# Layer-norm shift products of a cross-attention block: one column per product against one row of 512 columns

## The reference

```python
q, kv = _ln(queries, q_norm_g, q_norm_b), _ln(tokens, kv_norm_g, kv_norm_b)
qp = q @ in_proj_w[:D].T + in_proj_b[:D]
kp = kv @ in_proj_w[D:2*D].T + in_proj_b[D:2*D]
vp = kv @ in_proj_w[2*D:].T + in_proj_b[2*D:]
scores = einsum('bhld,bhtd->bhlt', qh, kh) / sqrt(hd) - spatial_scale * dist + spatial_offset
attn_out = einsum('bhlt,bhtd->bhld', softmax(scores), vh)
x = queries + attn_out @ out_proj_w.T + out_proj_b
h = gelu(_ln(x, mlp_norm_g, mlp_norm_b) @ mlp_w1.T + mlp_b1)
x = x + h @ mlp_w2.T + mlp_b2
```

## Time and profile before

| | us |
|---|---|
| median of 3 runs | 1252.32 (1252.31 to 1252.36) |
| the profiled execution | 1252.47 |
| its span, first to last instruction | 1250.6 |
| PE busy | 1220.2 (98%) |
| PE weight loads | 819.0 (65%) |
| DVE busy | 993.6 (79%) |
| ACT busy | 851.3 (68%) |
| POOL busy | 992.0 (79%) |

### The profile page before, as it was taken

One profiled execution on the slowest core, in us unless ns is written; L12 is line 12 of the kernel. 1 busy time (PEld: TensorE's weight loads), 2 busy tenths in 40 slices (PEclk: granted clock), 3 DMA queues, 4 the chain that ended last, 5 costly groups with the idle time before them and its releaser, 6 DMA issues.

```text
span 1250.6 us, 27744 instructions
## 1 busy us (share of the span) xinstructions
PE 1220.2 (98%) x9424; PEld 819.0 (65%) x9424; DVE 993.6 (79%) x2656; ACT 851.3 (68%) x1914; POOL 992.0 (79%) x1286
## 2 busy tenths in 40 slices
PE   9888988999999999999999999999999999999998
PEld 6656455666667666666666676666666666666664
DVE  5799998888878888888888989888888787778321
ACT  5867757676877677676767677776767677676331
POOL 5478897989898898989898998989898987767320
PEclk9788999999999999999999999999999999999999
DMA  6699999888999898998999998998889897879543
GB/s 185 197 188 208 224 224 195 192 189 209 209 194 222 180 214 198 193 203 201 198 205 218 180 223 182 202 203 203 194 206 208 195 208 176 173 170 180 142 113 123
DMA packets 468686, 241.69 MB, mean 193 GB/s; under 512 B 384048, under 2 KB 408896, under 8 KB 468544
## 3 DMA queue, kind: packets, MB, share of 16 engines
q1 hardware_dynamic: 468544, 239.91, 85.6%
HBM read 109.66 MB, written 12.58 MB: 98 GB/s over the span
## 4 chain that ended last, share of the span: by engine, by line
PE 86%; DVE 8%; issue 2%; ACT 1%; POOL 1%; DMA 1%; SPq 0%; POOLq 0%; DVEq 0%; ACTq 0%
PE ps_up L630 26%; PE ps_down L645 26%; PE ps_qk L566 12%; PE ps_vo L590 6%; PE ps_vo L587 6%; PE ps_s L601 5%; PE ps_pv L615 4%; DVE p_nat L1071 1%; DVE soft L1054 1%; PE ps_down L510 1%; DVE w L999 1%; DVE w L1005 1%; DVE x_nat L1031 1%; PE ps_down L541 0%; DVE qk_parts L1045 0%
## 5 line engine op out<-in xcount | busy, mean ns | idle before, releaser
L1248 POOL TENSOR_SCALAR p_nat<-soft,row_inv 128x256 f16<-128x256 f32 x512 | 332.1, 658 | 61.2 <-DVE row_inv L1065 59.4
L630 PE MATMUL ps_up<-hT,w 128*128 128x256 f16 x3072 | 377.2, 273 | 3.1 <-ACT u L805 2.7
L645 PE MATMUL ps_down<-w,hid 128*128 128x512 f16 x1536 | 372.9, 379 | 0.8 <-DVE hid L1103 0.4
L630 PEld LDWEIGHTS ps_up<-hT,w 128*128 128x128 f16 x3072 | 300.3, 98 | 93.2 <-ACT u L805 3.2
L773 ACT ACTIVATE soft<-soft,neg_max 128x256 f32<-128x256 f32 x512 | 255.2, 500 | 117.2 <-DVE neg_max L1054 116.2
L1054 DVE CUSTOM_DVE_ANT_0 soft<-ps_s,soft,factor 128x256 f32<-128x256 f32 x512 | 225.4, 476 | 116.7 <-PE ps_s L601 115.9
L1071 DVE SCALAR_TENSOR_TENSOR p_nat<-soft,row_inv,p_nat 128x256 f16<-128x256 f32 x512 | 297.6, 620 | 2.1 <-POOL p_nat L1248 1.9
L1256 POOL TENSOR_SCALAR soft<-dist,scale_neg,offset 128x512 f32<-128x512 f32 x256 | 244.3, 954 | 14.0 <-DVE p_nat L1071 13.6
L645 PEld LDWEIGHTS ps_down<-w,hid 128*128 128x128 f16 x1536 | 148.6, 97 | 132.4 <-DMA w<-x_scratch 1.4
L805 ACT ACTIVATE u<-ps_up,bias,up_scale 128x256 f32<-128x256 f32 x256 | 142.3, 556 | 124.9 <-PE ps_up L630 121.5
L1264 POOL TENSOR_SCALAR hid<-u,hid_scale 128x1024 f16<-128x1024 f32 x64 | 77.3, 1208 | 105.0 <-ACT u L811 105.0
(11 more groups left out here) (122 smaller groups left out, 1569.5 us busy)
## 6 DMA issues: line engine op xcount, KB each, us to landing
w<-x_scratch SPq DMA_DIRECT2D x256, 256.0 KB, 3.1
stack<-qk_parts SPq DMA_DIRECT2D x256, 96.0 KB
raw<-in_ctx SPq DMA_DIRECT2D x32, 256.0 KB, 3.4
raw<-in_x SPq DMA_DIRECT2D x32, 256.0 KB, 3.1
c_stage<-in_w SPq DMA_DIRECT2D x32, 256.0 KB, 3.6
x<-in_x SPq DMA_DIRECT2D x32, 256.0 KB, 3.5
out<-x SPq DMA_DIRECT2D x32, 256.0 KB, 3.2
tok_rows<-in_tok_xy SPq DMA_DIRECT2D x16, 256.0 KB, 4.4
```

Source lines behind the costliest of these rows:

```text
L630: mm = e.matmul(ps_up[s % 2][:, 0:L], w_1_sb[:, wp, k, m * P:(m + 1) * P], hT[:, b % 2, :, xp * KT + k, :], start=(k, wp, xp) == (0, 0, 0) ...
L645: mm = e.matmul(ps_down[tt][:], hid[:, chunk % HID_RING, i, hp, tt * P:(tt + 1) * P], w_2_sb[:, s % W2_RING, wp, :], start=(m == 0 and (hp ...
L1248: mine = e.tensor_scalar(p_nat[:, nat, HI, lc, :], soft[:, ring, lc, :], row_inv[:, ring, lc:lc + 1], 1.0, ALU.mult, ALU.mult)
```

## The change

It makes the shift products as rows. The stationary operand is now the single column of shifts, the moving operand is the whole 512-column weight row of one 128-row quarter, and the result is one row of 512 outputs. K, Q and V take 4 products each instead of 16, the MLP weight 16 instead of 64; the MLP chunks' rows lie on partitions 0, 32, 64 and 96 of their bank. The columns are read in the order of `by_column`, a step of 128 numbers between neighbours, so that the four numbers of one partition stand together in the row. ACT copies the row to SBUF (`bias_row`, `bias_rows_1`), and a DMA scatters it over the 128 partitions (`bias_turn`, `bias_turn_1`), from where DVE reads it as before. The row tiles lie in memory that other tiles use, and so `dist_square` and `load_residual` gain a wait for the scatter.

V's shift product moves from slots -2, 0 and 2 to slot -3, DVE's step for the MLP bias from slot 19 to 21. The unread products are placed anew: `warm` makes 10, 1, 1, 12 and 6 products instead of 10, 3, 10, 8, 2 and 8, and `keep_busy` starts in slot 0 instead of 7, writes `ps_pv` before slot 9, and counts a shift-product step as 4 units instead of 8. One more unread product (`clear_rows`) writes the MLP rows' bank in slot 0.

```diff
+        row_kv = sb("row_kv", [1, D], F32, at["x1"] + KT * D * 4)
+        row_q = sb("row_q", [1, D], F32, at["x1_n"])
+        rows_1 = sb("rows_1", [P, D], F32, at["x1"] + (KT + 1) * D * 4)
...
+            def bias_turn(sec):
+                gate.wait_ge(s_row, AT[sec] + 1)
+                e.dma_start(bias_qkv[:, sec * KT:(sec + 1) * KT], (row_q if sec == SEC_Q else row_kv)[:]).then_inc(s_rowd[sec], DMA)
+
+            def bias_turn_1():
+                gate.wait_ge(s_row, ROW_1)
+                for c in range(N_CHUNKS):
+                    e.dma_start(bias_1[:, c * CH:(c + 1) * CH], rows_1[32 * c:32 * c + 1, :]).then_inc(s_rowd_1, DMA)
...
-                gate.wait_ge(s_mkept, DMA)
-                gate.wait_ge(s_colsum, 1)
+                if t >= KT:
+                    gate.wait_ge(s_rowd_1, N_CHUNKS * DMA)
...
+                for sec, at_slot in ((SEC_K, -25), (SEC_Q, -24), (SEC_V, -1)):
+                    if slot == at_slot:
+                        bias_turn(sec)
+                if slot == 18:
+                    bias_turn_1()
...
-            def weight_bias(sec, quarters):
+            def by_column(w):
+
+                return w.rearrange("p (m q) -> p q m", m=KT)
...
                 gate.wait_ge(s_cols, DMA)
                 b_ln = B_Q if sec == SEC_Q else B_KV
-                for k in quarters:
...
-                    for m in range(KT):
-
-                        col = sec * KT + m
-                        mm = e.matmul(ps_bias[sec][:, col:col + 1], w_stage[sec][:, k, m * P:(m + 1) * P],
-                                      cols_sb[:, b_ln + k:b_ln + k + 1], start=((k, m) == (0, 0)), stop=((k, m) == (KT - 1, KT - 1)))
-                if KT - 1 in quarters:
...
+                if sec == SEC_V:
+                    gate.wait_ge(s_row, ROW_K)
                 for k in range(KT):
-                    mm = e.matmul(ps_bias[sec][:, col:col + 1], w_stage[sec][:, k, m * P:(m + 1) * P],
-                                  cols_sb[:, b_ln + k:b_ln + k + 1], start=(k == 0), stop=(k == KT - 1))
-                if m == KT - 1:
-                    mm.then_inc(s_brow)
...
-            def w1_bias(c, m):
-                col = c * CH + m
-                for k in range(KT):
-                    gate.wait_ge(s_wc[c % C_STAGES][k], n_staged(c))
-                    mm = e.matmul(ps_bias_1[:, col:col + 1], staged(c, k)[:, m * P:(m + 1) * P],
-                                  cols_sb[:, B_M + k:B_M + k + 1], start=(k == 0), stop=(k == KT - 1))
-                if m == CH - 1:
+                    if sec == SEC_V:
+                        gate.wait_ge(s_w[0], DMA)
+                    else:
+                        gate.wait_ge((s_wk if sec == SEC_K else s_wq)[k], DMA)
+                    mm = e.matmul(ps_bias[sec][0:1, :], cols_sb[:, b_ln + k:b_ln + k + 1], by_column(w_stage[sec][:, k, :]),
+                                  start=(k == 0), stop=(k == KT - 1))
+                mm.then_inc(s_brow)
+
+            def w1_bias(c, k):
+
+                gate.wait_ge(s_wc[c % C_STAGES][k], n_staged(c))
+                mm = e.matmul(ps_bias_1[32 * c:32 * c + 1, :], cols_sb[:, B_M + k:B_M + k + 1], by_column(staged(c, k)),
+                              start=(k == 0), stop=(k == KT - 1))
+                if k == KT - 1:
                     mm.then_inc(s_brow)
...
+            def clear_rows():
+
+                e.matmul(ps_bias_1[:], w_sec[SEC_K][:, HI, 0, 0:P], w_sec[SEC_K][:, HI, 0, :], start=True, stop=True)
...
-            def keep_busy(count):
-
-                gate.wait_ge(s_bo_all, 1)
+            def keep_busy(bank, count):
+
+                if bank is ps_down[0]:
+                    gate.wait_ge(s_bo_all, 1)
+                gate.wait_ge(s_wlo, AT[SEC_K] + 1)
                 for _ in range(count):
-                    e.matmul(ps_down[0][:], w_sec[SEC_K][:, HI, 0, 0:P], w_sec[SEC_K][:, HI, 0, :], start=True, stop=True)
...
+                    e.matmul(bank[:], w_sec[SEC_K][:, HI, 0, 0:P], w_sec[SEC_K][:, HI, 0, :], start=True, stop=True)
...
-                for at_slot, count in ((-32, 10), (-30, 3), (-8, 10), (-6, 8), (-3, 2), (-2, 8)):
+                for at_slot, count in ((-32, 10), (-30, 1), (-28, 1), (-8, 12), (-6, 6)):
...
-                for sec, quarters, at_slot in ((SEC_K, range(3), -31), (SEC_K, range(3, KT), -29), (SEC_Q, range(1), -29),
-                                              (SEC_Q, range(1, 3), -28), (SEC_Q, range(3, KT), -27)):
+                for sec, at_slot in ((SEC_K, -31), (SEC_Q, -29), (SEC_V, -3)):
                     if slot == at_slot:
-                        weight_bias(sec, quarters)
-                for m, at_slot in enumerate((-2, 0, 2, 2)):
-                    if slot == at_slot:
-                        value_bias(m)
+                        weight_bias(sec)
+                if slot == 0:
+                    clear_rows()
                 if slot == 4:
                     value_bias_out()
...
-                if 7 <= slot < DOWN:
+                if 0 <= slot < DOWN:
                     taken = 1 + (3 if due(slot, 9, GROUP, N_HG) else 0) + (6 if slot % 2 else 0) + (6 if slot >= UP else 0)
-                    taken += vo_done + (8 if due(slot, 1, ITEM, MT) else 0)
-                    keep_busy(max(0, SLOT_STEPS - taken))
+                    taken += vo_done + (4 if due(slot, 1, ITEM, MT) else 0)
+                    taken += 16 if slot == 4 else 0
+                    keep_busy(ps_pv if slot < 9 else ps_down[0], max(0, SLOT_STEPS - taken))
...
-                gate.wait_ge(s_bcol, BIAS_Q)
+                gate.wait_ge(s_row, ROW_Q)
...
+            def bias_row(sec):
+                gate.wait_ge(s_brow, AT[sec] + 1)
+                if sec == SEC_V:
+                    gate.wait_ge(s_rowd[SEC_K], DMA)
+                e.activation((row_q if sec == SEC_Q else row_kv)[:], ps_bias[sec][0:1, :], ACT.Copy).then_inc(s_row)
+
+            def bias_rows_1():
+                gate.wait_ge(s_brow, 3 + N_CHUNKS)
+                gate.wait_ge(s_mkept, DMA)
+                gate.wait_ge(s_colsum, 1)
+                e.activation(rows_1[0:97, :], ps_bias_1[0:97, :], ACT.Copy).then_inc(s_row)
...
+                gate.wait_ge(s_rowd[SEC_Q], DMA)
...
+                for sec, at_slot in ((SEC_K, -26), (SEC_Q, -24), (SEC_V, -2)):
+                    if slot == at_slot:
+                        bias_row(sec)
+                if slot == 17:
+                    bias_rows_1()
...
-                gate.wait_ge(s_brow, AT[sec] + 1)
-                e.tensor_tensor(bias_qkv[:, part], ps_bias[sec][:, part], cols_sb[:, B_IN + sec * KT:B_IN + (sec + 1) * KT], ALU.add).then_inc(s_bcol)
+                gate.wait_ge(s_rowd[sec], DMA)
+                e.tensor_tensor(bias_qkv[:, part], bias_qkv[:, part], cols_sb[:, B_IN + sec * KT:B_IN + (sec + 1) * KT], ALU.add).then_inc(s_bcol)
...
-                gate.wait_ge(s_brow, 3 + N_CHUNKS)
-                e.tensor_tensor(bias_1[:], ps_bias_1[:, 0:MT], cols_sb[:, B_1:B_1 + MT], ALU.add).then_inc(s_bcol)
+                gate.wait_ge(s_rowd_1, N_CHUNKS * DMA)
...
-                if slot == 19:
+                if slot == 21:
                     bias1_columns()
```

More of the change, by code:

```diff
@@ L967, in bias_v_spread @@
             def bias_v_spread():
-                gate.wait_ge(s_brow, AT[SEC_V] + 1)
+                gate.wait_ge(s_rowd[SEC_V], DMA)
                 gate.wait_ge(s_wsq, WSQ[3])
                 part = slice(SEC_V * KT, (SEC_V + 1) * KT)
-                e.tensor_tensor(bias_qkv[:, part], ps_bias[SEC_V][:, part], cols_sb[:, B_IN + SEC_V * KT:B_IN + (SEC_V + 1) * KT],
+                e.tensor_tensor(bias_qkv[:, part], bias_qkv[:, part], cols_sb[:, B_IN + SEC_V * KT:B_IN + (SEC_V + 1) * KT],
                                 ALU.add).then_inc(s_tv)
```

12 lines of the change are left out of this document (4 added, 8 removed).

## The result

| | before | after |
|---|---|---|
| median of the runs, us | 1252.34 (4 runs, 1252.31 to 1255.13) | 1260.1 (4 runs, 1259.58 to 1260.6) |
| ratio, 95% interval | | 1.0056 (1.0039 to 1.0074) |
| the profiled execution, its span | 1252.47, 1250.6 | 1260.6, 1258.8 |
| granted clock, mean of the span | 0.986 | 0.997 |

The change makes the kernel slower by 0.56%, some 7.8 us. I had forecast 5 us less, and the result lies above my range.

The account below looks back on a forecast made before the run. Chained waits bound the start, DVE's pace 58 to 176 us, PE the rest. Start 2.4 plus slots 2.6 gave 5.0 us off 1252.47, and with the median 0.15 lower 1247.3 us; range 1242.5 to 1255.0.

Parts of the forecast that it names:

- Prices: Cost of one 512-column row product on PE, taken from L541: 0.9 us at full clock, 1.8 at half.
- Rival (2): PE's stepped read halves the stream, 1.8 us a product even at full clock: slower, 1254.8 us; chance 0.15.
- The MLP rows: Rival (2)'s term for w1 steps: 0.9 us more each, 14 in all, of which 0.4 was counted.
- The start: Before slot 0: the forecast gained 2.4 us; Rival (2) lost 4.2, from K and Q 1.6 and V 2.6.
- the slots' gain: Slots 0 to 30: 2.6 us in the forecast, of which Rival (2) kept 2.1.
- The clock rises during the first product: K's rows at 6.2 us: PE's clock rises in their first product, so four take 4.5 us, done at 10.7.
- Rival (1): Narrow rows do not raise PE's clock; the start loses 1.6 us, the slots keep 2.1: 1251.8 us; chance 0.20.
- No 0.50 after 50 us: Sign that the forecast is right: PE's granted clock never reads 0.50 after 50 us.
- V's rows, 3.6 us at full clock: V's rows, ahead of a K projection that started at 33.9 us: 3.6 us, hidden; at 7.2 not hidden.
- What is late next is the scatter: ACT's `dist_square` waits for Q's scatter, landing at 20.2 to 22.9 us; Q's high parts start at 22 to 24.6.
- the slots' 2.6: Slots 0 to 30: 1.8 at O's total, 1.2 at the bias, 0.6 other idleness, less 1.0 for unread products.
- rival (3): DVE, 96% busy from 58 us, eats the slots' gain, leaving 0.4 beside the start's 2.4: 1249.5 us; chance 0.15.

Follow-up runs that it names:

- Experiment 1: Changed kernel with all weight rows read in natural order, ACT's row copy making the scatter's order; 1249.04 us, ratio 0.9970 to before.
- experiment 4: Measurement in the changed kernel: MLP weight chunks read with steps of 1, 2, 4, 8 numbers, unread fp16 products with steps up to 128; 1271.43 us, one run.
- experiment 9: Measurement in the changed kernel: MLP weight chunks and unread fp16 products read in 16-byte steps or short runs with jumps, one chunk plain; 1263.44 us, one run.
- experiment 5: Changed kernel with only K's, Q's and V's rows in natural order, the MLP weight's rows still stepped; 1253.61 us, ratio 1.0006 to before.
- experiment 8: Experiment 1 with Q's row in memory not otherwise used then, so `dist_square` does not wait for its scatter; 1248.71 us, ratio 0.9964 to before.
- experiment 10: Experiment 1 with `keep_busy` starting in slot 7 instead of 0; 1249.85 us, ratio 0.9977 to before.
- Experiment 7: Experiment 1 with 26 unread products instead of 6 in slot -6, ahead of Q's projection; 1247.28 us, ratio 0.9953 to before.

## Why the prediction was wrong

**The step that failed is in "Prices".** "Of the new form ... no row exists. Its bounds: half of that at the lower end ..., twice as much at the upper. I take 0.9 and 1.8, the nearest row." At full clock the upper bound was the true value: 1.78 us a product where the sum has 0.9, and nearly all rows ran at full clock. The form differed from the nearest row, L541, in two things, the narrow stationary operand and the step of the moving one. Experiment 1 shows that the first is free (0.90 to 0.91 us a product), experiments 4 and 9 that with the second each number costs a line of its own. With the natural order the same change gives -3.8 us of the -5.0 forecast.

**Rival (2) named the mechanism, and its sum was too small by 5.3 us** (1254.8 against 1260.1). The Trainium skill (SBUF — State Buffer, Door 1: The DMA port swizzle) says that a 16-byte line is what a read pays for, and that at least two hits a line keep it free. The trace agrees with the line as the unit. Two hits a line are free here in fp32 (1.06 against 1.02) but not in fp16 (0.47 against 0.24). The same section of the Trainium skill gives figures for a free stride, 4 numbers in fp32 and 8 in bf16 (fp16 here, of the same width). They don't hold for PE's moving operand here either: a step of 4 in fp32 doubles the product (1.96 against 1.02), and in fp16 already a step of 4 does.

The rival's prices failed in two terms, which make 4.5 of the 5.3 us:
- The MLP rows. I counted 0.4 of 14 us, because "PE had 9 us free in 58 to 122 and gets more by the clock". They cost 4.3 (experiment 5 against 1). The 14 us were right, (1.90 - 1.02) x 16; but these slots also hold the unread products, which fill each slot to 16 units, and the table counts a step as 4 units, 0.96 us. PE was busy 57.91 of 64 us with plain rows, 6 us free and not 9 or more, and the 14 us went into that stretch and little around it. The free time of the kernel as changed was what the price had to be held against.
- The start. I counted 4.2 lost and it was 4.8 against before, and 8.0 against experiment 1 (46.36 against 38.40; 6.1 to 8.0 over experiments 1, 5, 8 and 10, whose K, Q and V rows are plain). K's rows take 3.4 us more than plain (7.12 - 1.02 - 2.73), Q's 3.5 and V's, which stand ahead of a K projection, 2.7; of these 9.6 us 8.0 reach slot 0.

The rival also kept 2.1 us of the slots' gain. Up to the first MLP product it did not come (see below).

**The clock, point by point.** "The clock rises during the first product" was right or a little late. Where the ten unread products still take 4.45 us (experiments 7 and 8), K's rows take 3.71 and 3.81 against 3.59 at full clock, so the rise falls into their first product; in after (4.25) and in experiment 1 (3.63) it came already during the ten. That it also rises during one-column-wide rows is shown by V's, in after and in experiment 1. Rival (1) falls. "No 0.50 after 50 us" was right as well (1.00 in both stretches). What I had not seen is the place between K's and Q's projections, where PE waits 5.2 us for DVE and the clock falls: Q's projection at 2.72 instead of 1.47 us and V's rows partly at half speed. My "V's rows, 3.6 us at full clock" took no account of it. Experiment 7 fills the wait, and both run at full clock again.

**The start's chain.** With plain rows the foretold places are nearly met: "the copy of Q's total at 16 to 17 us" was 15.85, `dist_square` behind the scatter at 20.47 lies inside "20.2 to 22.9", and the start gains 3.15 us where I had 2.4. That agreement is weak: the scores of slot 0 stand at 38.40, 38.88, 40.24 and 39.22 us in experiments 1, 5, 8 and 10, and at 41.55 and 39.95 in two executions with the columns, so one profile can't place the start's gain. But "What is late next is the scatter" was wrong: experiment 8 takes its wait away and nothing moves. DVE's chain of Q's gain, norm and low parts is late there. The scatter of Q's row landed after 2.0 us in after and 3.3 with plain rows, where I had 2.3 to 5.0.

**Slots 0 to 30.** "DVE's wait at 44 us below 2 us" was right: 1.51 us at 47.30 in after, 1.52 in experiment 1, against 3.37. The first MLP product with plain rows is at 173.25 instead of the 171 forecast: the start brings 3.15 and the slots 176.20 - 173.25 - 3.15 = -0.2, so up to there the slots' 2.6 did not come, as far as these two executions can tell; another 1.35 of the span's 4.3 was gained behind 173 us. DVE sets the pace of the slots (61.88 of 64 us from 58 to 122), and what a shorter wait gives is idle time at the next, as rival (3) had it; that the gain went there is read from busy times and was not tested by itself.
